# A graph network kernel: sums by source begun in the scatter stage, in chunks of 384 rows, and a first stage with less in it

## The chip, the cores and the metric

One core of one Trainium2 chip runs the whole program in one launch. The metric is the device time of that launch in microseconds (us). Times in the trace count from the start of the profiled span. PE is the engine for matrix products (PEld its weight loads), DVE the vector engine, ACT the activation engine, POOL the GpSimd engine, SP the engine that only issues DMAs here.

## The reference, cut to what matters

The graph has N = 3125 nodes and E = 53125 directed edges with 128 features each; `dst` is sorted, `src` is not. Four graph layers run one after the other. The change touches the preparation of the first two, which need for each node the sum of the edge rows that start in it and the sum of those that end in it:

```
edge_aggr = jnp.zeros((x.shape[0], edge_attr.shape[1]), dtype=x.dtype)
edge_aggr = edge_aggr.at[row].add(edge_attr).at[col].add(edge_attr)     # row = src, col = dst
node_features = jnp.concatenate([x, edge_aggr], axis=1)
h = jax.nn.relu(node_features @ W1 + b1)
```

Before each layer the node rows are normalised (mean and variance over the 128 features), which is why statistics of x are made in the same preparation.

## The kernel before, in words

The edges are 415.04 tiles of 128, handled as 416 tiles: 208 pairs of tiles, or 104 groups of four tiles (`PAIRS`, `GROUPS`). The nodes are 25 blocks of 128. There are four stretches of interest, each closed by a barrier of all engines.

**First stage** (lines 410 to 520). Constants, index tables, clearing of the big tables, the first loads of edge rows. ACT and POOL clear `between`, a table of 20000 words per partition: POOL in two memsets of 2800 and 9400 words (L456, L458), ACT the other 7800 (L440). DVE makes the tables from the indices; PE turns them and then runs 16 products of ones (`stream_ones`, L380), which serve no result. SP loads edge rows into a ring of eight groups and issues the large DMA that zeroes the end of each block's place in DRAM (L426, L429), then the last four of the ring's loads.

**Scatter stage** (`place_and_count`). For each group, PE works out the place of each edge row in a table in DRAM that is kept by the block of its source node (`rank`, L897 to L901). DVE reads the ranks (`own_rank`, L830), ACT turns the base of the next group out of PSUM (`base_of_next`, L789), DVE turns ranks into places (`place`, `place_whole`, L839), and POOL writes the rows to those places, four indirect DMAs to a group (L765). For each pair, DVE makes wide one-hots (`hots`, L817), ACT narrow ones (`lows`, L782 and L785), PE multiplies them (L917 to L926), and DVE adds the product to `between` and `by_dst` two pairs later (`collect`, L849 and L851). ACT writes the key of a row beside it (`key_in_row`, L775). Each engine runs a list in program order. `which_block` of DVE (L824) waits for the newest rank, and `rank` waits for the base that ACT makes. Every pair begins on PE with products of ones: 3 of them, in every 32nd pair 16.

**Stage of the sums by source** (`sum_blocks`). The rows of each block are read back from DRAM, 18 tiles of 128 rows for each of 24 blocks and 9 for the last: 441 tiles in 74 reads of up to six, in a ring of four buffers. SP issues a read when PE has finished with the buffer (L1101), DVE makes a one-hot of the keys (`where`, L1120), PE adds up (L1170), DVE adds the sum by destination (`add_dst`, L1112). Beside it DVE makes the statistics of x (L1063, L1136), and ACT checks the 25 blocks of `between` (L1153).

**The rest** (from L1187 on): the four layers. The change leaves it as it is, except that some of its semaphores are shared with a branch that isn't taken.

Of the kernel before, what the change touches and what calls it, by code (L numbers as in the profile page):

```python
# [12 lines left out]
F32 = mybir.dt.float32  # L13
# [66 lines left out]
WARM_SHORT = 12  # L80
LAST_BANK = 7
WARM_EVERY = 32


class Signal:
# [6 lines left out]
    def __init__(self, make):  # L92
        self.make, self.on_path, self.base = make, {}, {}

    @property
    def h(self):
        branch = Signal.path is not None
        if branch not in self.on_path:
            self.on_path[branch] = self.make()
        return self.on_path[branch]  # L100
# [44 lines left out]
def build(nc, x, src, dst, ea, l0, l1, l2, l3, out):  # L145
    ctx = ExitStack()
    with ctx:
# [7 lines left out]
        def signal(name):  # L155
# [3 lines left out]
            return Signal(make)  # L159
# [95 lines left out]
        bounds = sb("bounds", [1, 2, NB])  # L255
        over = sb("over", [1, 2, NB])
# [22 lines left out]
        tab_row = sb("tab_row", [1, 2, 2, ST * P], I32)  # L279
        tab_bc = sb("tab_bc", [P, 2, 2, ST * P])  # L280

        shifts = [sb(f"shift{k}", [P, SLOTS_OF[k], GS[k]]) for k in range(2)]
# [15 lines left out]
        junk = grid_space.take([P, NP], U8)  # L298
        excess = grid_space.take([P, NB])
# [91 lines left out]
        POOL_FIRST, POOL_SECOND = 2800, 9400  # L391
# [18 lines left out]
        with nc.Block() as block:  # L410
            @on(block.sync)
            def _(sp):
# [18 lines left out]
                for g in range(EARLY, ROWG):  # L431
                    load_group(sp, g)

            @on(block.scalar)
            def _(act):
# [77 lines left out]
            def _(pe):  # L513
# [8 lines left out]
                stream_ones(pe, LAST_BANK, WARM_UP)  # L522
# [126 lines left out]
        pair_done = signal("pair_done")  # L649
        taken = signal("taken")  # L650
# [68 lines left out]
        def place_and_count():  # L719
# [15 lines left out]
            with nc.Block(no_gpsimd_drain=True) as block:  # L735
                @on(block.sync)
                def _(sp):
                    for g in range(ROWG, GROUPS):
# [6 lines left out]
                        if g == 6 * ROWG:  # L745
                            sp.wait_ge(vec.h, vec.at(1))
                            sp.dma_start(x_nm[:, 0:NB - 1, :], x[0:(NB - 1) * P, :].rearrange("(b p) f -> p b f", p=P)).then_inc(loaded.h, 16)
                            sp.dma_start(x_nm[0:NLAST, NB - 1, :], x[(NB - 1) * P:N, :]).then_inc(loaded.h, 16)
                    sp.wait_ge(loaded.h, loaded.at(16 * 23))
# [19 lines left out]
                def _(act):  # L769
# [16 lines left out]

                    def base_of_next(g):
                        act.wait_ge(ranks_read.h, ranks_read.at(g + 1))
                        act.activation(bases[:, (g + 1) % 2, :], acc[0:1, R_AT + RANKS:R_AT + RANKS + NK], ACT.Copy).then_inc(based.h, 1)  # L789
# [4 lines left out]
                    for i in range(PAIRS):  # L794
# [4 lines left out]
                        if i % PG == 1 and g + 1 < GROUPS:  # L799
                            base_of_next(g + 1)  # L800

                @on(block.vector)
                def _(dve):
# [54 lines left out]
                    for i in range(PAIRS + 2):  # L858
                        g = i // PG
                        if i % PG == 0 and g < GROUPS:  # L860
                            place(g)
                        if i < PAIRS:
                            hots(i)
                        if i % PG == 0 and g < GROUPS:
# [7 lines left out]
                        if i == 4 * ROWG * PG:  # L872
                            dve.wait_ge(tail_zero.h, tail_zero.at(32))
                            dve.memset(x_nm[:, NB - 1, :], 0.0).then_inc(vec.h, 1)
                    dve.memset(odd[:, 3:4], 0.0)
                    dve.tensor_scalar(bounds[:, 0, 0:NB - 1], iota[0:1, 0:NB - 1], float(CAP), float(FILLED), ALU.mult, ALU.add)
# [1717 lines left out]
```

## Time and profile before

| | |
|---|---|
| median of 3 runs | 1464.97 us (1463.71 to 1466.68) |
| the profiled execution's own time | 1461.87 us |
| its span | 1460.0 us |
| first stage | 0 to 22.6 us |
| scatter stage | 22.6 to 558.7 us |
| stage of the sums by source | 558.7 to 685.4 us |
| the rest | 685.4 to 1460.0 us |

The stages follow each other with barriers, so what one stage is shortened or lengthened by moves everything behind it. Within a stage the engines run side by side, and the stage is as long as the one that ends last.

### The profile page before, as it was taken

Reading aid. Unit: us, or ns where it says so; the run is one execution under the profiler, and the core shown is the slowest. Engines: PE = TensorE matmul, PEld = TensorE weight load, DVE = VectorE, ACT = ScalarE, POOL = GpSimd, SP = SyncE. Lnnn points to the kernel's source line nnn. Section 1 sums busy time; section 2 is a strip of 40 time slices with the busy share of each in tenths; the row PEclk is TensorE's granted clock in tenths of the full one; section 3 lists DMA queues with packets and bytes.
Section 4 is the critical chain, followed back from the end, with each engine's and each line's share of the span. In section 5 each row is a group of like instructions: output and inputs, shape, how many; then the busy total and the mean of one; then the engine's idle time right before and its main releaser. Section 6 shows DMA issues by size and latency. Waiting matters only on the chain. (4 is left out here: it accounts for less than half of the span.)

```text
span 1460.0 us, 32667 instructions
## 1 busy us (share of the span) xinstructions
PE 1248.2 (85%) x9632; PEld 906.7 (62%) x9633; DVE 880.1 (60%) x2762; ACT 554.3 (38%) x1458; POOL 808.4 (55%) x844
## 2 busy tenths in 40 slices
PE   5888888888888887887789998999988898988986
PEld 3555555555555556886469996477766666666664
DVE  6777777787877876665785448244444433443434
ACT  5444544444445447940241104233322222222221
POOL 5777777777777771000000001777777777777770
PEclk9999999999999999999799998899999999999996
DMA  7533335333333325875500003655555555455422
GB/s 230 135 104 106 104 108 148 101 104 104 103 108 108 102 67 177 240 240 162 48 1 2 1 2 105 166 153 154 158 155 154 154 151 142 136 149 142 134 75 56
DMA packets 198505, 174.71 MB, mean 120 GB/s; under 512 B 48724, under 2 KB 171078, under 8 KB 198246
## 3 DMA queue, kind: packets, MB, share of 16 engines
q1 hardware_dynamic: 171752, 118.36, 30.1%
q0 software_dynamic: 26624, 54.79, 13.0%
q8 instruction: 61, 1.00, 0.3%
q14 instruction: 68, 0.56, 0.2%
HBM read 134.89 MB, written 38.16 MB: 119 GB/s over the span
## 5 line engine op out<-in xcount | busy, mean ns | idle before, releaser
L2132 POOL DMA_INDIRECT between<-p_table,src_g x416 | 397.2, 955 | 474.1 <-DMA p_table<-n_nm 347.6
L380 PE MATMUL acc<-ones_b 128*128 128x512 bf16 x1606 | 426.3, 386 | 31.4 <-PEq L1396 12.4
L765 POOL DMA_INDIRECT rows_by_block<-h_t,mean_bc x312 | 299.8, 961 | 109.7 <-issue 77.4
L380 PEld LDWEIGHTS acc<-ones_b 128*128 128x128 bf16 x1606 | 142.5, 99 | 132.6 <-issue 39.0
L917 PE MATMUL acc<-n_nm 128*128 128x384 bf16 (+1 forms) x832 | 140.8, 291 | 86.6 <-DVE n_nm L817 85.8
L2204 ACT ACTIVATE between<-acc 128x256 f32<-128x256 f32 x208 | 79.8, 383 | 355.3 <-PE acc L2252 348.2
L849 DVE TENSOR_TENSOR between<-between,acc 128x600 f32 x208 | 161.3, 775 | 61.5 <-issue 49.8
L2163 DVE TENSOR_TENSOR between<-acc,between 128x256 f32<-128x256 f32 x208 | 87.8, 422 | 169.2 <-DMA between<-p_table,src_g 108.6
L2277 PE MATMUL acc<-w_msg,between 128*128 128x128 f32 x832 | 185.5, 305 | 0.0
L2263 PEld LDWEIGHTS acc<-between 128*128 128x128 f32 x832 | 129.6, 198 | 82.6 <-issue 58.9
L2263 PE MATMUL acc<-between 128*128 128x24 f32 x832 | 134.6, 243 | 49.5 <-DVE agg_sum L2172 49.0
L917 PEld LDWEIGHTS acc<-n_nm 128*128 128x128 bf16 x832 | 66.3, 97 | 163.5 <-DVE n_nm L817 134.3
L817 DVE TENSOR_SCALAR n_nm<-iota_w,agg_sum 128x600 bf16<-128x600 f16 x416 | 153.5, 409 | 0.0
L782 ACT ACTIVATE away<-iota_b,agg_sum 128x128 bf16<-128x128 bf16 x416 | 140.8, 385 | 0.0
L2277 PEld LDWEIGHTS acc<-w_msg,between 128*128 128x128 f32 x832 | 127.0, 193 | 0.1
L789 ACT ACTIVATE bases<-acc 1x26 f32<-1x26 f32 x104 | 18.9, 182 | 265.1 <-DVE agg_sum L830 262.8
L1170 PE MATMUL acc<-n_nm,h_t 128*128 128x128 f32 x882 | 108.2, 280 | 12.7 <-DVE n_nm L1120 12.2
L765 POOL DMA_INDIRECT rows_by_block<-agg_sum,mean_bc x104 | 99.7, 959 | 32.5 <-issue 25.5
L2252 PE MATMUL acc<-ident,between 128*128 128x128 f32 x416 | 114.3, 276 | 0.0
L1170 PEld LDWEIGHTS acc<-n_nm,h_t 128*128 128x128 f32 x882 | 101.7, 192 | 19.4 <-DVE n_nm L1120 18.9
L2172 DVE TENSOR_TENSOR agg_sum<-agg_sum,acc 128x24 f32 x208 | 37.4, 180 | 117.8 <-issue 60.1
L785 ACT ACTIVATE n_nm<-away,ones 128x256 bf16<-128x256 bf16 x208 | 105.6, 508 | 6.8
(194 smaller groups left out, 1942.7 us busy)
## 6 DMA issues: line engine op xcount, KB each, us to landing
h_t<-rows_by_block SPq DMA_DIRECT2D x73, 387.0 KB, 3.7
between<-in_edge_attr SPq DMA_DIRECT2D x207, 128.0 KB
h_t<-in_edge_attr SPq DMA_DIRECT2D x78, 256.0 KB
between<-in_dst SPq DMA_DIRECT2D x51, 288.0 KB
between<-p_table,src_g POOLq DMA_INDIRECT x416
agg_sum<-in_edge_attr SPq DMA_DIRECT2D x25, 256.0 KB
rows_by_block<-h_t,mean_bc POOLq DMA_INDIRECT x312
rows_by_block<-x_nm SPq DMA_DIRECT2D x1, 4644.0 KB, 18.6
```

Source lines behind the costliest of these rows:

```text
L380: pe.matmul(acc[:, bank * BANK:(bank + 1) * BANK].rearrange("p (a n) -> p a n", n=P), ones_b[:, :], ones_b[:, :].rearrange("p (a n) -> p a ...
L765: pool.indirect_dma_start(rows_by_block, bass.IndirectOffsetOnAxis(ap=place_in_table[:, t:t + 1], axis=0), row_group(g)[:, j, :], None).th ...
L782: act.activation(away[:, h + j, :], iota_b[:, :], ACT.Abs, scale=-1.0, bias=lo_s[:, 2 * i + j:2 * i + j + 1])\
L785: act.activation(low_hot[:, h:h + 2, :], away[:, h:h + 2, :], ACT.Relu, scale=-1.0, bias=ones[:, 0:1]).then_inc(lows_made.h, 1)
L817: ins = dve.tensor_scalar(wide_hot[:, i % HOTB * 2 + j, :], iota_w[:, :], key_w[:, t:t + 1], None, ALU.is_equal)
L849: dve.tensor_tensor(between[:, :, bass.ds(first, W)], between[:, :, bass.ds(first, W)], acc[:, o:o + NB * WS].rearrange("p (b w) -> p b w" ...
L917: pe.matmul(acc[:, to:to + (b1 - b0) * WS].rearrange("p (b w) -> p b w", w=WS)[:, :, 0:W], low_hot[:, h + j, :], wide_hot[:, h + j, b0 * W ...
L1170: last = pe.matmul(acc[:, o:o + P], rows_in_block[:, q, j, 0:D], hot_in_block[:, q, j, :], start=is_first and j == 0, stop=is_last and j = ...
L2132: pool.indirect_dma_start(got[:, q, j * D:(j + 1) * D], None, p_table, bass.IndirectOffsetOnAxis(ap=src_g[:, n * G + j:n * G + j + 1], axi ...
L2252: last = pe.transpose(acc[:, o:o + P], rows[:, i, j, :], ident[:, :])
L2263: last = pe.matmul(acc[:, o:o + W], relued[:, i % MR, j, :], onehot[:, i * G + j, :], start=j == 0, stop=j == G - 1)
L2277: last = pe.matmul(acc[:, o:o + P], turned[:, i % MR, j * P:(j + 1) * P], w_msg[:, 2, :], start=False, stop=True)
```

## The change: what it does

1. In the scatter stage, from group 29 on, the first 9 of the 18 tiles of each of 24 blocks are read back and summed while later rows are still being scattered. A chunk is 3 tiles (384 rows) of one block, 72 chunks in all, one to a group. SP loads it (`load_chunk`), ACT makes its one-hot (`hots_of_chunk`: three Abs and one Relu), PE sums it (`sum_chunk`) and ACT copies the result out of PSUM to `home` (`take_chunk`). In the second and third round over the blocks PE first adds what `home` already holds, by a product with the identity.
2. PE's list there: `rank` comes ahead of the products of ones; they go to the bank of the pair, behind the wait for it (`taken`); a pair with a chunk has 1 of them, not 3.
3. The stage of the sums reads 225 tiles in 50 reads, not 441 in 74. The load of x moves into it from the scatter stage. DVE adds `by_dst` to `home` there once (3072 words) and joins the last 11 blocks of `between` by ten bitwise ors of 800 words, so that ACT checks 15 blocks, not 25. PE starts it with 6 products of ones, not 16.
4. First stage: POOL clears in 26 pieces of 400 words without waiting for anyone, ACT 9600 words, not 7800; 12 products of ones, not 16; the last four ring loads go to the next stage.
5. The first group's `place_whole` comes ahead of its one-hots on DVE.

```diff
+CT = 3
+CROWS = CT * P
+CRING, CHOTS = 3, 2
+CHUNK_LOAD, CHUNK_HOT, CHUNK_SUM, CHUNK_TAKE = 32, 29, 30, 31
+CHUNKS = EC // KC - CHUNK_LOAD
+BY_CHUNK = [min(NB - 1, CHUNKS - c * (NB - 1)) for c in range(-(-CHUNKS // (NB - 1)))]
...
-        POOL_FIRST, POOL_SECOND = 2800, 9400
+        POOL_PIECE, POOL_PIECES = 400, 26
...
-                clear(between_words[:, POOL_FIRST + POOL_SECOND:])
+                clear(between_words[:, POOL_PIECE * POOL_PIECES:])
...
-                pool.wait_ge(vec.h, vec.at(6))
-                pool.memset(between_words[:, 0:POOL_FIRST], 0.0)
-                pool.wait_ge(idx_read.h, idx_read.at(1))
-                pool.memset(between_words[:, POOL_FIRST:POOL_FIRST + POOL_SECOND], 0.0)
+                for k in range(POOL_PIECES):
+                    pool.memset(between_words[:, k * POOL_PIECE:(k + 1) * POOL_PIECE], 0.0)
...
-                stream_ones(pe, LAST_BANK, WARM_UP)
+                stream_ones(pe, LAST_BANK, WARM_SHORT)
...
+                    def load_chunk(m):
+                        if m >= CRING:
+                            sp.wait_ge(chunk_summed.h, chunk_summed.at(m + 1 - CRING))
+                        row = m % (NB - 1) * CAP + m // (NB - 1) * CROWS
+                        sp.dma_start(chunk_rows[:, m % CRING, :, :], rows_by_block[row:row + CROWS, :].rearrange("(p j) w -> p j w", j=CT))\
+                          .then_inc(chunk_in[m % CRING].h, 16)
...
+                    def hots_of_chunk(m):
+                        act.wait_ge(chunk_in[m % CRING].h, chunk_in[m % CRING].at(16 * (m // CRING + 1)))
+                        if m >= CHOTS:
+                            act.wait_ge(chunk_summed.h, chunk_summed.at(m + 1 - CHOTS))
+                        h = chunk_hot[:, m % CHOTS, :, :]
+                        for j in range(CT):
+                            act.activation(h[:, j, :], iota[:, :], ACT.Abs, scale=-1.0, bias=chunk_rows[:, m % CRING, j, D:KW]).then_inc(chunk_away.h, 1)
+                        act.wait_ge(chunk_away.h, chunk_away.at(CT * (m + 1)))
+                        act.activation(h, h, ACT.Relu, scale=-1.0, bias=ones[:, 0:1]).then_inc(chunk_hots.h, 1)
+
+                    def take_chunk(m):
+                        act.wait_ge(chunk_summed.h, chunk_summed.at(m + 1))
+                        o, b = IDLE_BANK * BANK, m % (NB - 1)
+                        act.activation(home[:, b * P:b * P + P], acc[:, o:o + P], ACT.Copy).then_inc(chunk_taken.h, 1)
...
                             base_of_next(g + 1)
+                        if i % PG == 1 and 0 <= g - CHUNK_HOT < CHUNKS:
+                            hots_of_chunk(g - CHUNK_HOT)
+                        if i % PG == 0 and 0 <= g - CHUNK_TAKE < CHUNKS:
+                            take_chunk(g - CHUNK_TAKE)
...
+                    def sum_chunk(m):
+                        pe.wait_ge(chunk_hots.h, chunk_hots.at(m + 1))
+                        if m >= 1:
+                            pe.wait_ge(chunk_taken.h, chunk_taken.at(m))
+                        o = IDLE_BANK * BANK
+                        again = m >= NB - 1
+                        if again:
+                            b = m % (NB - 1)
+                            pe.matmul(acc[:, o:o + P], ident[:, :], home[:, b * P:b * P + P], start=True, stop=False)
+                        for j in range(CT):
+                            last = pe.matmul(acc[:, o:o + P], chunk_rows[:, m % CRING, j, 0:D], chunk_hot[:, m % CHOTS, j, :],
+                                             start=j == 0 and not again, stop=j == CT - 1)
+                        last.then_inc(chunk_summed.h, 1)
...
-                        stream_ones(pe, IDLE_BANK, WARM_UP if i % WARM_EVERY == WARM_EVERY - 1 else WARM_PAIR)
                         if c == 0 and g + 1 < GROUPS:
                             rank(g + 1)
+                        with_chunk = c == 0 and 0 <= g - CHUNK_SUM < CHUNKS
+                        if with_chunk:
+                            sum_chunk(g - CHUNK_SUM)
+                        if i >= PRING:
+                            pe.wait_ge(taken.h, taken.at(i + 1 - PRING))
+                        stream_ones(pe, at_bank(i) // BANK, WARM_UP if i % WARM_EVERY == WARM_EVERY - 1 else WARM_CHUNK if with_chunk else WARM_PAIR)
...
+                done = CT * sum(b < k for k in BY_CHUNK)
+                for j in range(done, n, LR):
...
+                        if r == 2:
+                            dve.tensor_tensor(home[:, 0:(NB - 1) * P], home[:, 0:(NB - 1) * P], agg_dst[:, 0:(NB - 1) * P], ALU.add)
```

**PE, one group of the scatter stage.** Before the change PE's list for a group reads as follows (L380 are the products of ones, L897 to L901 the rank, L917 to L926 the products of a pair).

```order
L380 MATMUL acc<-ones_b 128x512 x3
L897 MATMUL acc<-bases,ones 128x130
L888 MATMUL acc<-agg_sum,ones_b 128x104
L888 MATMUL acc<-agg_sum,ones_b 128x78
L888 MATMUL acc<-agg_sum,ones_b 128x52
L888 MATMUL acc<-agg_sum,ones_b 128x26
L901 MATMUL acc<-agg_sum,lower_b 128x104
L917 MATMUL acc<-n_nm 128x16x24 x2
L917 MATMUL acc<-n_nm 128x9x24 x2
L923 MATMUL acc<-agg_sum 128x24 x2
L926 MATMUL acc<-agg_sum,ones_b 128x24 x2
```

With the change, in a group of the second and third round over the blocks (L952 to L956 are the rank, L966 the identity product, L968 the chunk, L395 the ones, L989 on the pair):

```order
L952 MATMUL acc<-bases,ones 128x130
L943 MATMUL acc<-agg_sum,ones_b 128x104
L943 MATMUL acc<-agg_sum,ones_b 128x78
L943 MATMUL acc<-agg_sum,ones_b 128x52
L943 MATMUL acc<-agg_sum,ones_b 128x26
L956 MATMUL acc<-agg_sum,lower_b 128x104
L966 MATMUL acc<-home,ident 128x128
L968 MATMUL acc<-x_nm 128x128 x3
L395 MATMUL acc<-ones_b 128x512
L989 MATMUL acc<-n_nm 128x16x24 x2
L989 MATMUL acc<-n_nm 128x9x24 x2
```

The rank has moved to the front, and the chunk stands between it and the pair's own products, in place of two of three products of ones.

**ACT, one group of the scatter stage.** Before (L789 is the base, L782 and L785 the one-hots of a pair, L775 the key):

```order
L789 ACTIVATE bases<-acc 1x26
L782 ACTIVATE away<-iota_b,agg_sum 128x128 x2
L785 ACTIVATE n_nm<-away,ones 128x256
L775 ACTIVATE h_t<-agg_sum 128x4
L782 ACTIVATE away<-iota_b,agg_sum 128x128 x2
L785 ACTIVATE n_nm<-away,ones 128x256
```

With the change (L833 is the base, L819 and L821 the chunk's one-hot, L808 and L811 the pair's, L801 the key, L826 the copy of the chunk of the group before):

```order
L833 ACTIVATE bases<-acc 1x26
L819 ACTIVATE x_nm<-iota,x_nm 128x128 x3
L821 ACTIVATE x_nm<-x_nm,ones 128x384
L808 ACTIVATE away<-iota_b,agg_sum 128x128 x2
L811 ACTIVATE n_nm<-away,ones 128x256
L801 ACTIVATE h_t<-agg_sum 128x4
L826 ACTIVATE home<-acc 128x128
L808 ACTIVATE away<-iota_b,agg_sum 128x128 x2
L811 ACTIVATE n_nm<-away,ones 128x256
```

The one-hot of the chunk that PE sums next stands ahead of the pair's one-hots, and the copy of the chunk before it stands behind them.

**DVE, the stage of the sums, its sixth to eighth read.** With the change (L1208 makes the one-hot of a read, L1228 is a bitwise or, L1200 adds the sum by destination):

```order
L1208 TENSOR_TENSOR n_nm<-iota,h_t 128x384
L1228 TENSOR_TENSOR mean_bc<-between 128x800
L1208 TENSOR_TENSOR n_nm<-iota,h_t 128x768
L1228 TENSOR_TENSOR mean_bc<-mean_bc,between 128x800
L1200 TENSOR_TENSOR agg_sum<-acc,home 128x128
L1208 TENSOR_TENSOR n_nm<-iota,h_t 128x384
L1228 TENSOR_TENSOR mean_bc<-mean_bc,between 128x800
```

Reads of six and of three tiles alternate, and each of ten reads is followed by an or, where before each read had six tiles and a short statistics instruction behind it in the middle part.

## Rows read from the trace of the kernel before

**Rows 1.** Busy us (x instructions) per engine, granted clock, DMA share, GB/s; three stages.

```profile
0.00:22.64 22.64, 8.33 (x26) 3.74 (x27) 14.85 (x30) 13.42 (x4) 11.70 (x12) 1.00 0.90 282
22.64:558.75 536.11, 442.40 (x3510) 274.96 (x3511) 417.48 (x1308) 255.88 (x832) 399.53 (x416) 1.00 0.37 107
558.75:685.37 126.62, 113.17 (x898) 103.52 (x898) 84.06 (x162) 78.00 (x53) 0.00 (x0) 0.99 0.77 231
```

**Rows 2.** Timeline, first stage: start, us, engine, line, what, idle before.

```profile
7.00 7.93 POOL L458 MEMSET between<- 128x9400 f32 x1 [0.60 <-DVE n_nm L489]
7.46 6.69 ACT L440 ACTIVATE between<-ones 128x7800 f32<-128x7800 f32 x1
8.80 6.24 DVE L492 TENSOR_SCALAR win_f<-mean_bc 1x208 f32<-1x208 f32 x1
...
16.09 5.12 PE L380 MATMUL acc<-ones_b 128*128 128x512 bf16 x16
...
17.99 4.23 SPq L405 DMA_DIRECT2D agg_sum<-in_edge_attr  x2
...
22.66 0.44 DVE L824 TENSOR_TENSOR agg_sum<-iota,agg_sum 128x104 bf16<-128x104 f32 x2 [3.14 <-PEq L410]
```

**Rows 3.** Timeline of POOL: its first and its last (416th) scatter.

```profile
26.22 1.15 POOL L765 DMA_INDIRECT rows_by_block<-h_t,mean_bc  x1 [11.29 <-ACT h_t L775]
...
555.71 0.96 POOL L765 DMA_INDIRECT rows_by_block<-agg_sum,mean_bc  x1 [0.31 <-issue]
```

**Rows 4.** Timeline, one group of the scatter stage with PE, DVE and ACT.

```profile
520.13 0.29 PEld L897 LDWEIGHTS acc<-bases,ones 1*128 1x128 f32 x2 [0.42 <-issue]
520.70 0.21 PE L901 MATMUL acc<-agg_sum,lower_b 128*128 128x104 bf16 x1
520.80 0.67 PE L917 MATMUL acc<-n_nm 128*128 128x384 bf16 x4
520.95 0.27 DVE L824 TENSOR_TENSOR agg_sum<-iota,agg_sum 128x104 bf16<-128x104 f32 x1 [0.59 <-PE acc L901]
...
521.74 0.81 PE L380 MATMUL acc<-ones_b 128*128 128x512 bf16 x3
...
523.95 0.26 DVE L830 TENSOR_TENSOR agg_sum<-acc,agg_sum 128x104 f32<-128x104 f32 x1
524.24 0.18 ACT L789 ACTIVATE bases<-acc 1x26 f32<-1x26 f32 x1 [2.31 <-DVE agg_sum L830]
...
524.32 0.68 ACT L782 ACTIVATE away<-iota_b,agg_sum 128x128 bf16<-128x128 bf16 x2
...
525.03 0.51 ACT L785 ACTIVATE n_nm<-away,ones 128x256 bf16<-128x256 bf16 x1
...
525.45 0.19 ACT L775 ACTIVATE h_t<-agg_sum 128x4 f32<-128x4 f32 x1
```

**Rows 5.** Timeline, a late POOL start, and a pair with 16 products of ones.

```profile
506.74 0.76 DVE L849 TENSOR_TENSOR between<-between,acc 128x600 f32 x1
...
507.53 0.95 POOL L765 DMA_INDIRECT rows_by_block<-agg_sum,mean_bc  x1 [1.10 <-issue]
...
510.18 3.61 PE L380 MATMUL acc<-ones_b 128*128 128x512 bf16 x16
```

**Rows 6.** Lines in the stage of the sums: count, busy us, mean ns, idle before.

```profile
L1120 DVE TENSOR_TENSOR n_nm<-iota,h_t 128x768 f32<-128x768 f32 x74 | 70.4, 951 | 42.1 <-DMA h_t<-rows_by_block 41.8
...
L1214 ACT ACTIVATE w_msg<-acc 128x128 f32<-128x128 f32 x1 | 0.3, 277 | 2.8 <-PE acc L1206 2.8
```

**Rows 7.** Timeline, stage of the sums: first read, PE on a read, last read.

```profile
561.85 0.96 DVE L1120 TENSOR_TENSOR n_nm<-iota,h_t 128x768 f32<-128x768 f32 x1 [1.45 <-DMA h_t<-rows_by_block]
...
569.32 1.41 PEld L1170 LDWEIGHTS acc<-n_nm,h_t 128*128 128x128 f32 x12 [0.25 <-DVE n_nm L1120]
...
683.09 0.56 DVE L1120 TENSOR_TENSOR n_nm<-iota,h_t 128x384 f32<-128x384 f32 x1 [1.26 <-DMA h_t<-rows_by_block]
```

**Rows 8.** Windows: the thinnest five us of PE in the sums.

```profile
645.00:650.00 5.00, 3.38 (x28) 3.00 (x26) 2.29 (x6) 0.00 (x0) 0.00 (x0) 1.00 0.83 242
```

More of the change, by code:

```diff
@@ L254, in build @@
         bases = sb("bases", [1, 2, NK])
-        bounds = sb("bounds", [1, 2, NB])
-        over = sb("over", [1, 2, NB])
+        chunk_space = Space(x_nm[:, :, :].rearrange("p b f -> p (b f)")[:, (CAP - FILLED) // P * KW if FILLED else 6 * KW:], F32)
+        chunk_rows = chunk_space.take([P, CRING, CT, KW])
+        chunk_hot = chunk_space.take([P, CHOTS, CT, P])
+        bounds = chunk_space.take([1, 2 + len(BY_CHUNK), NB])
+        over = chunk_space.take([1, 2 + len(BY_CHUNK), NB])
+        counts_at = chunk_space.take([1, len(BY_CHUNK), NB])
         low_bound = sb("low_bound", [P, 1])
@@ L276, in build @@
         b1_row = sb("b1_row", [P, H2])
-        tab_row = sb("tab_row", [1, 2, 2, ST * P], I32)
-        tab_bc = sb("tab_bc", [P, 2, 2, ST * P])
-        shifts = [sb(f"shift{k}", [P, SLOTS_OF[k], GS[k]]) for k in range(2)]
+        home = sb("home", [P, NP])
+        general_space = Space(home[:, :], F32)
+        tab_row = general_space.take([1, 2, 2, ST * P], I32)
+        tab_bc = general_space.take([P, 2, 2, ST * P])
+        shifts = [general_space.take([P, SLOTS_OF[k], GS[k]]) for k in range(2)]
         win_f = sb("win_f", [1, PAIRS])
@@ L649, in build @@
         pair_done = signal("pair_done")
+        chunk_in = [signal(f"chunk_in{q}") for q in range(CRING)]
+        chunk_away = signal("chunk_away")
+        chunk_hots = signal("chunk_hots")
+        chunk_summed = signal("chunk_summed")
+        chunk_taken = signal("chunk_taken")
         taken = signal("taken")
@@ L861, in _ @@
                             place(g)
+                        if i == 0:
+                            place_whole(g)
                         if i < PAIRS:
                             hots(i)
-                        if i % PG == 0 and g < GROUPS:
+                        if i % PG == 0 and 0 < g < GROUPS:
                             place_whole(g)
@@ L873, in _ @@
                             dve.wait_ge(tail_zero.h, tail_zero.at(32))
+                            dve.memset(over[:, :, :], 0.0)
                             dve.memset(x_nm[:, NB - 1, :], 0.0).then_inc(vec.h, 1)
                     dve.memset(odd[:, 3:4], 0.0)
+                    for c, n in enumerate(BY_CHUNK):
+                        dve.tensor_scalar(bounds[:, 2 + c, 0:n], iota[0:1, 0:n], float(CAP), float((c + 1) * CROWS), ALU.mult, ALU.add)
                     dve.tensor_scalar(bounds[:, 0, 0:NB - 1], iota[0:1, 0:NB - 1], float(CAP), float(FILLED), ALU.mult, ALU.add)
@@ L883, in _ @@
                     dve.tensor_tensor(over[:, 1, :], bases[:, GROUPS % 2, 0:NB], bounds[:, 1, :], ALU.is_gt)
+                    for c, n in enumerate(BY_CHUNK):
+                        dve.tensor_tensor(over[:, 2 + c, 0:n], counts_at[:, c, 0:n], bounds[:, 2 + c, 0:n], ALU.is_lt)
                 @on(block.tensor)
@@ L937, in place_and_count @@
             away_made.passed(EC)
-            loaded.passed(16 * 23)
+            for s in (chunk_hots, chunk_summed, chunk_taken):
+                s.passed(CHUNKS)
+            chunk_away.passed(CT * CHUNKS)
+            for q in range(CRING):
+                chunk_in[q].passed(16 * len(range(q, CHUNKS, CRING)))
+            loaded.passed(16 * 21)
             vec.passed(2)
@@ L1151, in _ @@
                 def _(act):
-                    for b in range(NB):
-                        act.activation(junk[:, :], between[:, b, :], ACT.Relu, bias=low_bound[:, :], accum_out=excess[:, b:b + 1]).then_inc(checked.h, 1)
-                        if b < NB - 1:
+                    for b in range(ALONE + 1):
+                        if b == ALONE:
+                            act.wait_ge(united.h, united.at(NB - ALONE - 1))
+                        of = between[:, b, :] if b < ALONE else mean_bc[:, 2 * EC:2 * EC + NP // 4].bitcast(U8)
+                        act.activation(junk[:, :], of, ACT.Relu, bias=low_bound[:, :], accum_out=excess[:, b:b + 1]).then_inc(checked.h, 1)
+                        if b < ALONE:
                             act.wait_ge(checked.h, checked.at(b + 1))
```

109 lines of the change are left out of this document (70 added, 39 removed).

## The prediction

> **What bounds the kernel now.** I read the table by stage first, then the timeline inside each stage that the change touches. The table [rows 1] gives 22.64 us to the first stage, 536.1 to the scatter stage, 126.6 to the sums by source; the rest is left alone. The first stage ends with SP: its last two loads run from 17.99 for 4.23 us, to 22.22, and DVE begins the next stage at 22.66 [rows 2]. Before that DVE lost time: an instruction on 208 elements took 6.24 us and ended at 15.04, just behind POOL's 9400-word memset, which ended at 14.93 [rows 2].
>
> In the scatter stage POOL is busy 399.5 us and runs from 26.22 to 555.71 + 0.96 = 556.67 [rows 1, 3]. That is 530.45 us for 416 scatters, 1.275 each with the 0.30 us that stands before one, so 5.10 us to a group. POOL never rests, and bounds the stage. But PE, DVE and ACT are close behind. The group shown [rows 4] is one link of a loop: PE's rank (from 520.13 to 520.91) lets DVE go on, DVE's chain ends with L830 at 524.21, ACT's base follows at 524.24. A change that puts work into this loop must be judged by the loop and not by ACT's 255.9 us of 536 [rows 1].
>
> In the stage of the sums DVE waits 41.8 us for rows [rows 6], DMA moves 231 GB/s [rows 1], and reads follow each other every (683.09 - 561.85)/73 = 1.66 us [rows 7]. The reads bound it.
>
> **First stage.** SP's last loads leave it. What is left: ACT's clearing, 6.69 us for 7800 words from 7.46 [rows 2], becomes 6.69 x 9600/7800 = 8.23 and ends at 15.7. PE's last burst of ones has 12 and not 16, and begins some 6 us earlier. DVE no longer sits behind one memset, but each of its instructions may meet a piece: 7.93 x 400/9400 = 0.34 us. From 15.04 (end of the stalled one) DVE has work until 19.5 (estimate: 22.66 less its idle 3.14 [rows 2]), 4.5 us, and without the stall it would begin this near 9.3; with ten meetings at half to a whole piece it ends at 15.5 to 17. I take 16.6 for the last engine and 17.0 for the next stage's start: 5.6 us earlier. Bounds: 16.1 (ACT alone) and 22.6 (nothing gained). The moved loads are wanted only from group 4 on, some 20 us into the stage; they are issued at its start and cost nothing. The Trainium skill, SBUF — State Buffer, section "SBUF: two separate sides", says that DVE in a two-port mode and POOL take a shared port pair for a whole instruction; the trace agrees in the 6.24 us above, and by that rule a piece of 0.34 us is the most that one meeting costs.
>
> POOL began 3.56 us after the stage did (26.22 against 22.66); `place_whole` ahead of the first one-hots takes about the 0.67 us of two of them off. POOL begins at 19.9.
>
> **Scatter stage.** Per chunk ACT gains three Abs, a Relu on 384, and a copy; PE gains three tiles and from the 25th chunk on an identity product, and loses two products of ones. Counted as work ACT would hold: it waits 2.31 us before each base [rows 4]. But the order makes a longer loop. `sum_chunk(m)` on PE waits for `take_chunk(m-1)`. That copy stands on ACT behind the base, the chunk's one-hot, one pair's one-hots and the key. On PE the chunk stands ahead of both pairs of the group, and the next rank stands behind them. From a rank to the rank two groups on, this must be walked through:
> - DVE from rank to L830: 524.21 - 520.91 = 3.30 [rows 4].
> - ACT from L830 to the end of the copy: 0.03 to the base and 0.08 to the next start; three Abs 1.01 (0.71 from the first of two to the Relu [rows 4], one more 0.30); Relu on 384: 0.42 for 256 (525.03 to 525.45 [rows 4]) and 0.12 for 128 more, 0.54; the pair's one-hots 0.71 + 0.42; key 0.10; copy 0.28 as L1214 [rows 6]; 0.05 to PE. Together 3.22.
> - PE from there to the rank after next: three tiles 0.70 (12 loads for six tiles in 1.41 us [rows 7]), one product of ones 0.22 (3.61/16 [rows 5]), a pair 0.94 (520.80 to 521.74 [rows 4]), three ones 0.68, a pair 0.94, 0.05, the rank 0.78. Together 4.31, with the identity product 0.235 more, 4.55.
>
> The sum is 10.83 us for two groups, 5.42 a group, and 5.53 with the identity. POOL needs 5.10. So over 72 groups not POOL but this loop sets the pace: 24 x 5.42 + 48 x 5.53 = 395.5 us. In five of these groups (every 16th) stands the pair with 16 ones; 13 x 0.225 = 2.9 us each, now on the path, 14.6 together. PE waits in each such group, about 1.1 us before the chunk.
>
> The groups without a chunk get quicker, since the ones stand behind the rank now. Their shortest loop is 3.30 + 0.03 + 0.18 + 0.05 + 0.78 = 4.34 us; POOL's pace, at which they go now, is 5.10. I take 4.7. In 30 such groups the three engines run ahead of POOL, which later eats up this lead. The last group's places are ready at 19.9 + 30 x 4.7 + 2 (one burst) + 395.5 + 14.6 + 4.7 = 577.7, and with its four scatters (5.04) POOL ends at 582.7: 26.0 us later than the 556.67 of before. Left out as hidden: SP's chunk loads (half a read of six tiles to a group, issued two groups ahead; DMA share is 0.37 [rows 1] and would be near 0.5), and the small bounds and counts of DVE and ACT.
>
> Bounds: the free pace 4.34 to 5.10 (-10.8, +12); ACT's part 0.3 either way (0.15 x 72 = 10.8 either way), since no row has an Abs or a Relu of these shapes.
>
> **Stage of the sums.** 225 of 441 tiles, 50 reads not 74, and x (3125 rows of 512 bytes, 1.6 MB) more. From below: the stage moved 231 GB/s x 126.6 = 29.2 MB; 225/441 of it is 14.9, with x 16.5, at 240 GB/s (231 to 242 [rows 1, 8]) 69 us, with 3.1 before the first read (561.85 - 558.75) and 2 behind the last, 74. From above: 50 reads at the 1.66 us of the larger ones, 83, and 5, 88. DVE: 84.1 us [rows 1] less 24 reads of 0.951 and 25 that shrink from 0.951 to 0.56, less 32.6, plus ten ors of 800 at about 0.99 ((0.951 - 0.56)/384 us an element) and one sum of 3072 at 3.3, gives 65; it comes close to the reads in the part with the ors. I take 80, nearer the middle: 46.6 less than 126.6.
>
> **Sum.** 1461.87 + 26.0 - 46.6 = 1441.3 (the 5.6 of the first stage is inside the 26.0). The median of before lies 3.1 over the profiled execution; so 1444.
>
> **The rivals.**
> *POOL still bounds the scatter stage.* If the copy and one-hots of a chunk cost less than half of what I put, or the lead is enough, POOL runs 530.45 us from 19.9 on to 550.4, 6.3 earlier than before. 1461.87 - 6.3 - 46.6 + 3.1 = 1412. For it: ACT's 2.31 us of waiting [rows 4]. Against: the wait for the copy is in the code, and 5.42 stands against 5.10.
>
> *POOL's pieces starve DVE in the first stage.* 26 x 0.34 is 8.8 us back to back; if DVE gets no gap, the stage is as long as before: 5.6 more, 1450.
>
> *ACT's part is longer.* Each 0.1 us on it adds 0.05 x 72 = 3.6. With 0.6 more: 1444 + 21.6 = 1466, and nothing is gained.
>
> *DVE blocks POOL, slower.* A scatter began 0.80 us late (1.10 of idle for 0.30) and began when DVE's L849 (506.74 + 0.76 = 507.50) was over, at 507.53 [rows 5]. Now the two keep step, and this is rare. If DVE out of step blocks one scatter in each group, POOL needs 5.10 + 0.80 = 5.90, in 104 groups 613.6, to 633.5: 1461.87 + 76.8 - 46.6 + 3.1 = 1495. It decides from 0.51 us a group on (583.4/104 = 5.61). Against it: of the 530.45 us all but some 6 are 416 x (0.96 + 0.30). The Trainium skill tells of this in SBUF — State Buffer, "SBUF: two separate sides": a DVE instruction in a two-port mode keeps the cores of GpSimd from writing DMA descriptors. [...]
>
> *PE's clock falls in the thinner sums.* PE would be busy near two thirds of the time. The thinnest five us of before had 3.38 busy at clock 1.00 [rows 8], which speaks against it. At half speed 225 tiles of 2 x 0.235 are 106 us, with 5 more 111: 1444 + 31 = 1475.
>
> **How the numbers follow.** The forecast as summed 0.74; POOL bound 0.08; starved DVE 0.08; longer ACT part 0.05; blocked POOL 0.03; clock 0.02. The forecast's own range, from its bounds taken together (11, 11, 7 and 2 us, root of squares 17 to 19), is 1426 to 1462. Leaving out half of the extremes on both sides the range is 1417 to 1463; POOL-bound and blocked POOL lie outside. A measurement tells 0.2%, 2.9 us, from no change: faster (below 1462.0) 0.86, within 0.07, slower 0.07.
>
> **What would show it.** Right: in groups 30 to 101 POOL idles 0.3 to 0.5 us more per group, and the rank follows the rank by 5.4 to 5.5 us; PE waits for ACT before the chunk; ACT hardly waits for L830; before group 30 scatters lag behind their places. The next stage begins near 17, the sums near 585, and last 80. Wrong: scatters every 1.26 us to the end; PE's wait before the chunk absent; a stage of the sums over 90 or under 72 us.

## The result, and the profile after

The changed kernel takes 1486.36 us (median of 4 runs, 1484.47 to 1488.85), the kernel before beside it 1465.83 (1463.71 to 1469.23): ratio 1.0139, 95% interval 1.0112 to 1.0166. It is slower by 20.5 us where 1444 was forecast, and it lies outside the range. The profiled execution's own time is 1488.85, its span 1487.0.

The windows of the changed kernel, by its three stages (columns as in [rows 1]):

```profile
0.00:22.14 22.14, 8.41 (x22) 3.52 (x23) 17.58 (x30) 14.92 (x4) 11.04 (x36) 1.00 0.88 289
22.14:629.80 607.66, 511.66 (x3894) 369.97 (x3895) 401.75 (x1315) 375.03 (x1195) 400.98 (x416) 0.92 0.41 115
629.80:714.46 84.66, 64.44 (x456) 57.31 (x456) 61.90 (x150) 47.44 (x33) 0.00 (x0) 0.92 0.65 196
```

The first stage gives 0.5 us (22.64 - 22.14), the scatter stage costs 71.5 (607.66 - 536.11), the sums give 42.0 (126.62 - 84.66), the rest, 772.5 us, gives 2.1: together the span is 27.0 us longer (1487.0 against 1460.0). The granted clock of the scatter stage is 0.92, where it was 1.00, and POOL is as busy as before.

The first stage, from the timeline of the changed kernel:

```profile
1.91 9.75 POOL L469 MEMSET between<- 128x400 f32 x26
2.60 9.15 DVE L492 CAST iota<-iota_i 128x128 f32<-128x128 int32 x1
2.73 9.01 DVE L493 CAST part<-part_i 128x1 f32<-128x1 int32 x1
...
7.47 8.19 ACT L453 ACTIVATE between<-ones 128x9600 f32<-128x9600 f32 x1
...
16.56 5.30 PE L395 MATMUL acc<-ones_b 128*128 128x512 bf16 x12
```

Both casts end by 11.75, just behind the last of 26 pieces (1.91 + 9.75 = 11.66). DVE's whole chain begins only then. The twelve ones wait for it, begin at 16.56 (16.09 before) and end at 21.86, and with them the stage. They take 0.44 us each, twice the 0.22 of [rows 5], and so 5.30 together, more than the 5.12 of the sixteen before.

Timeline of POOL in the changed kernel, its first and last scatter:

```profile
25.00 1.15 POOL L791 DMA_INDIRECT rows_by_block<-h_t,mean_bc  x1 [13.34 <-ACT h_t L801]
...
626.79 0.95 POOL L791 DMA_INDIRECT rows_by_block<-agg_sum,mean_bc  x1 [0.30 <-issue]
```

The run of the scatters is 627.74 - 25.00 = 602.7 us; 562.8 were forecast (582.7 - 19.9), and 530.45 it was [rows 3].

Waits of the changed kernel: who waited for what, us in total, times, longest:

```profile
POOL rows_by_block L791 <- DVE mean_bc L887: 83.7, 41, 6.7
...
PE acc L966 <- ACT home L826: 51.5, 24, 2.2
...
PE acc L968 <- ACT home L826: 25.3, 12, 2.4
```

PE waits for the copy `home` 36 times in 72 chunks, 76.8 us in all, 2.13 each: in every second group. POOL in turn waits 83.7 us for its places, which in the kernel before were 5.8 us between 24 and 550. Two groups in the timeline of the changed kernel (L956 ends a rank, L826 is the copy, L966 and L968 the chunk, L989 and L995 a pair, L395 the ones):

```profile
395.85 0.48 PE L952 MATMUL acc<-bases,ones 1*128 1x130 f32 x2
...
396.42 0.21 PE L956 MATMUL acc<-agg_sum,lower_b 128*128 128x104 bf16 x1
...
397.64 0.67 PE L989 MATMUL acc<-n_nm 128*128 128x384 bf16 x4
...
400.81 0.21 PE L956 MATMUL acc<-agg_sum,lower_b 128*128 128x104 bf16 x1
...
402.78 0.26 ACT L826 ACTIVATE home<-acc 128x128 f32<-128x128 f32 x1
...
403.18 0.46 PE L966 MATMUL acc<-home,ident 128*128 128x128 f32 x2 [2.16 <-ACT home L826]
...
404.64 1.21 PE L989 MATMUL acc<-n_nm 128*128 128x384 bf16 x4
...
405.64 0.92 PE L995 MATMUL acc<-agg_sum,h_t 128*128 128x24 f32 x4
...
406.46 1.29 PE L395 MATMUL acc<-ones_b 128*128 128x512 bf16 x3
...
408.60 0.48 PE L952 MATMUL acc<-bases,ones 1*128 1x130 f32 x2
```

The short group takes 4.39 us (396.42 to 400.81). In the long one PE stands idle for 2.16 us (a stand, below) and then makes the pair's products in 1.21 us, not 0.67. A rank's first product is 396.42 - 395.85 = 0.57 ahead of its L956, so the one begun at 408.60 has it at 409.17: 8.36 us, and 12.75 for both, where 11.07 were forecast. The windows of the same stretch show the clock:

```profile
402.00:404.00 2.00, 0.82 (x7) 0.85 (x8) 2.00 (x6) 1.94 (x7) 1.60 (x2) 1.00 0.11 35
404.00:406.00 2.00, 2.00 (x11) 1.30 (x10) 1.64 (x8) 1.78 (x7) 1.49 (x2) 0.51 0.35 60
406.00:408.00 2.00, 2.00 (x11) 1.15 (x12) 0.00 (x0) 1.97 (x8) 1.39 (x3) 0.63 0.83 272
408.00:410.00 2.00, 2.00 (x23) 1.85 (x22) 0.27 (x1) 0.52 (x2) 1.70 (x2) 1.00 0.21 66
```

PE is on its lower level, 1.2 GHz, in nearly all of the window behind the stand and most of the next, and back at 2.4 GHz in the last.

Not every stand is followed by this. The long group just before, and the windows there:

```profile
389.70 0.21 PE L956 MATMUL acc<-agg_sum,lower_b 128*128 128x104 bf16 x1
...
392.06 0.46 PE L966 MATMUL acc<-home,ident 128*128 128x128 f32 x2 [2.16 <-ACT home L826]
...
393.25 0.67 PE L989 MATMUL acc<-n_nm 128*128 128x384 bf16 x4
```

```profile
392.00:394.00 2.00, 1.94 (x16) 1.71 (x17) 1.97 (x7) 1.78 (x7) 1.70 (x2) 1.00 0.20 66
394.00:396.00 2.00, 2.00 (x19) 1.48 (x19) 0.56 (x3) 1.94 (x6) 1.39 (x3) 1.00 0.84 231
```

The stand is the same 2.16 us, but the pair's products take 0.67, and the group is over in 6.72 us (389.70 to 396.42): 11.11 for it and the short one behind it, which is the 11.07 of the forecast. Over the stage, the first pair behind a stand took 0.67 us in 14 of the 36 cases, 1.20 or 1.21 in 18, and something between in four. From one L956 to the next, 22 long groups take 1.4 to 2.95 us more than those at full clock do (6.50 early in the stage, 6.72 later; 9.3 and 9.52 where the sixteen ones stand), 42.95 us together. Without these the run of the scatters would be 602.74 - 42.95 = 559.8 us.

### The profile page after: what moved, and what is told of

It is laid out like the page before. It is cut to its first block and busy times, and to the rows that moved or that the text cites. A ratio compares the mean times of both kernels' runs of the same rounds, so it can differ in the third digit from the quotient of the medians.

```text
span 1487.0 us, 33072 instructions
## 1 busy us (share of the span) xinstructions
PE 1271.7 (86%) x9570; PEld 958.7 (64%) x9571; DVE 843.9 (57%) x2757; ACT 644.2 (43%) x1801; POOL 810.2 (54%) x868
## 5 line engine op out<-in xcount | busy, mean ns | idle before, releaser
L395 PE MATMUL acc<-ones_b 128*128 128x512 bf16 x1448 | 412.3, 403 | 32.3 <-PEq L1507 11.7
L395 PEld LDWEIGHTS acc<-ones_b 128*128 128x128 bf16 x1448 | 136.5, 102 | 130.9 <-issue 43.7
L897 DVE TENSOR_TENSOR between<-between,acc 128x600 f32 x208 | 161.5, 776 | 60.1 <-issue 56.8
L989 PE MATMUL acc<-n_nm 128*128 128x384 bf16 (+1 forms) x832 | 155.6, 314 | 0.1
L865 DVE TENSOR_SCALAR n_nm<-iota_w,agg_sum 128x600 bf16<-128x600 f16 x416 | 144.3, 388 | 0.0
L989 PEld LDWEIGHTS acc<-n_nm 128*128 128x128 bf16 x832 | 85.8, 105 | 86.2 <-issue 28.8
L808 ACT ACTIVATE away<-iota_b,agg_sum 128x128 bf16<-128x128 bf16 x416 | 141.1, 387 | 0.0
L833 ACT ACTIVATE bases<-acc 1x26 f32<-1x26 f32 x104 | 18.9, 182 | 214.7 <-DVE agg_sum L878 214.7
L872 DVE TENSOR_TENSOR agg_sum<-iota,agg_sum 128x104 bf16<-128x104 f32 x104 | 27.8, 268 | 142.4 <-PE acc L956 139.5
L811 ACT ACTIVATE n_nm<-away,ones 128x256 bf16<-128x256 bf16 x208 | 105.6, 508 | 6.8
L2387 PE MATMUL acc<-between 72*128 72x128 bf16 x416 | 91.4, 220 | 0.0
```

What stands on the lines that cost most here:

```text
L395: pe.matmul(acc[:, bank * BANK:(bank + 1) * BANK].rearrange("p (a n) -> p a n", n=P), ones_b[:, :], ones_b[:, :].rearrange("p (a n) -> p a ...
L808: act.activation(away[:, h + j, :], iota_b[:, :], ACT.Abs, scale=-1.0, bias=lo_s[:, 2 * i + j:2 * i + j + 1])\
L811: act.activation(low_hot[:, h:h + 2, :], away[:, h:h + 2, :], ACT.Relu, scale=-1.0, bias=ones[:, 0:1]).then_inc(lows_made.h, 1)
L865: ins = dve.tensor_scalar(wide_hot[:, i % HOTB * 2 + j, :], iota_w[:, :], key_w[:, t:t + 1], None, ALU.is_equal)
L897: dve.tensor_tensor(between[:, :, bass.ds(first, W)], between[:, :, bass.ds(first, W)], acc[:, o:o + NB * WS].rearrange("p (b w) -> p b w" ...
L989: pe.matmul(acc[:, to:to + (b1 - b0) * WS].rearrange("p (b w) -> p b w", w=WS)[:, :, 0:W], low_hot[:, h + j, :], wide_hot[:, h + j, b0 * W ...
```

## The experiments

**Theory.** Two things were paid: the loop through the copy of the chunk before, as forecast; and the lower clock behind many of the stands of 2.2 us, which wasn't. **Rival:** the loop alone, or the clock for want of work in all.

**The copy first.** ACT takes the chunk before at the head of a group, ahead of the base, and not behind the one-hots.

```diff
+                        if i % PG == 1 and 0 <= g - CHUNK_SUM < CHUNKS:
+                            take_chunk(g - CHUNK_SUM)
                         if i % PG == 1 and g + 1 < GROUPS:
                             base_of_next(g + 1)
...
-                        if i % PG == 0 and 0 <= g - CHUNK_TAKE < CHUNKS:
-                            take_chunk(g - CHUNK_TAKE)
```

> One move in ACT's list of the changed kernel: the copy of a chunk (take_chunk) stands ahead of the base of the same group's second pair, where ACT waits anyway, and no longer behind the next chunk's one-hot and a pair's one-hots. Theory of the loop (PE waits for the copy, then loses clock): the walk from a rank to the rank two groups on falls to 3.30 + 2.94 + 3.39 = 9.6 us, 4.8 a group, below POOL's 5.10; POOL runs 530 us from 25.0 on, PE no longer stands still before a chunk, its clock stays at 1.00 in the scatter stage, and the time is near 1414. Rival, DVE or the chunk loads hold POOL back: scatters go on having gaps, the scatter stage stays over 570 us and the time over 1450.

Measured: 1419.37 us (1416.94 to 1421.29), ratio to before 0.9672 (0.9635 to 0.9709). The waits of PE for `home` are gone (what is left is 39 waits for the chunk's one-hot, 24.4 us, the longest 1.1), and so is POOL's for its places (4.6 us in all). The windows of its stage show the clock at 0.98; it is 1.00 from 100 to 500 and 0.88 from 500 to 550, where PE runs out of work:

```profile
180.00:555.50 375.50, 328.38 (x2745) 243.77 (x2742) 278.11 (x892) 286.46 (x903) 283.84 (x294) 0.98 0.46 135
```

Its last scatter, in the timeline:

```profile
552.43 0.96 POOL L791 DMA_INDIRECT rows_by_block<-agg_sum,mean_bc  x1 [0.30 <-issue]
```

The scatters run 553.39 - 25.00 = 528.4 us: POOL bounds again. One place on ACT's list was worth 67 us (1486.36 - 1419.37); 1414 was expected.

**Ones in the wait.** ACT's list stays as in the changed kernel; PE gets five products of ones where it stood, and none behind. The wait for the pair's bank moves ahead of the chunk with them.

```diff
-                        if with_chunk:
-                            sum_chunk(g - CHUNK_SUM)
...
-                        stream_ones(pe, ..., WARM_CHUNK if with_chunk else WARM_PAIR)
+                        stream_ones(pe, ..., 5 if with_chunk else WARM_PAIR)
+                        if with_chunk:
+                            sum_chunk(g - CHUNK_SUM)
```

> The changed kernel, but a pair with a chunk has its products of ones (5, not 1) between the rank and the wait for the chunk, and none behind it: PE still waits for the copy, but is busy for 1.1 us of the wait. Theory that the clock makes the part of the loss that the sum of durations lacks: the clock stays near 1.00 in groups 30 to 101, groups follow each other every 5.3 to 5.5 us without a long one in two, the scatter stage takes some 555 to 565 us, the time is near 1440. Rival, the loop is longer for another reason than the clock: the stage stays near 600 us and the time near 1480.

Measured: 1446.63 us (1443.55 to 1451.25), ratio 0.9864 (0.9824 to 0.9904). The windows of the scatter stage:

```profile
180.00:576.00 396.00, 381.26 (x3024) 269.05 (x3024) 279.41 (x894) 285.57 (x904) 282.33 (x294) 1.00 0.46 128
```

PE in the timeline, three ranks that follow each other:

```profile
395.80 0.21 PE L956 MATMUL acc<-agg_sum,lower_b 128*128 128x104 bf16 x1
395.84 1.24 PE L395 MATMUL acc<-ones_b 128*128 128x512 bf16 x5
...
401.33 0.21 PE L956 MATMUL acc<-agg_sum,lower_b 128*128 128x104 bf16 x1
...
406.69 0.21 PE L956 MATMUL acc<-agg_sum,lower_b 128*128 128x104 bf16 x1
```

More products of no use, and 40 us less. The clock is 1.00, and two groups take 10.89 us (395.80 to 406.69). The forecast's 11.07 has a product of ones of 0.22 behind the chunk, which this kernel doesn't have on the path; without it 10.85 were forecast. The scatters run from 23.77 to 576.30, 552.5 us, 24 over the copy-first kernel. Of the 50.2 us to the changed kernel's 602.7, some 8 (an estimate: 36 x 0.22) are that product, and some 42 the clock, which agrees with the 42.95 counted above.

**Three ones behind the chunk** (`WARM_CHUNK = 3`). It tells the stand from want of work in all. It ran first on a chip on which the kernel before takes 1868.8 us (more on this below), and again on another beside the changed kernel.

> The changed kernel, with 3 products of ones in a pair with a chunk in place of 1, in their place behind the chunk. Theory A: PE's clock falls because of the stand of 2.2 us ahead of the chunk in every second group, which these ones don't shorten. Then the clock stays at 0.92 to 0.93, the loop has up to 0.45 us more for two groups, 72/2 x 0.45 = 16 us, and the time is 1490 to 1502. Rival: the clock falls because PE does too little in all in these groups; two more products a pair bring it back to 0.96, and with some 40 us less from the clock and 16 more of products the time is 1455 to 1470.

> The changed kernel with 3 products of ones behind the chunk, beside the changed kernel on one chip. As before: where the stand ahead of the chunk is what lowers the clock, the time is 0 to 16 us over the changed kernel's and the clock no higher; where PE's whole work in these groups is what counts, it is 15 to 30 us under it and the clock 0.95 or more.

> The changed kernel once more, so that the next run has it on its own chip. 1.014 of the kernel before on either chip.

Measured, all on one chip, with before at 1463.78: three ones 1505.06 (1502.6 to 1507.92), changed kernel again 1484.92 (1480.37 to 1488.4, ratio 1.0147, 1.0115 to 1.0178). PE was busy for 33.8 us more between 180 and the last scatter (391.47 against 357.70), and the clock there was 0.91 against 0.92. Timeline with three ones:

```profile
400.43 0.46 PE L966 MATMUL acc<-home,ident 128*128 128x128 f32 x2 [1.72 <-ACT home L826]
...
401.54 1.49 PE L395 MATMUL acc<-ones_b 128*128 128x512 bf16 x3
402.82 1.21 PE L989 MATMUL acc<-n_nm 128*128 128x384 bf16 x4
...
405.28 0.67 PE L989 MATMUL acc<-n_nm 128*128 128x384 bf16 x4
```

Ones behind the chunk don't help: the stand stays (35 of them, most of 1.7 to 2.1 us), the pair's products behind it came slow in 23 cases, and there the ones run at half speed themselves. In the changed kernel one such product took 0.63 us behind the stand, here three take 1.49: 0.86 more in 36 long groups bounds it at 31 us from above, and 20 were lost (1505.06 - 1484.92), 4 more than the 16 that were put as the most. The rival, which had 15 to 30 us less, falls. On the other chip the ratio was 1.0136 (1.0078 to 1.0194), with no changed kernel beside it.

**The order of PE alone.** The kernel before, with the rank ahead of the ones, and the ones in the pair's bank behind `taken`.

> The kernel before with PE's list changed alone: the rank ahead of the products of ones, these in the pair's own bank behind the wait for it. No chunks, first stage and sums as before. POOL bounds the stage, so the time stays within 0.2% of before (1463 to 1468); places should run ahead of their scatters by several groups at the end if the quicker loop (4.3 to 4.7 us a group) is real, and by 3 us as before if POOL's pace binds DVE through another way.

Measured: 1462.95 us, ratio 0.9970 (0.9947 to 0.9994). Part 2 of the change costs nothing and brings next to nothing; the cost is in the chunks. The quicker loop is real: in this trace the last L901 stands at 523.05, 33 us ahead of the end of the last scatter, where it was 11 before (545.48 and 556.67). In the changed kernel the groups ahead of the chunks go at 4.50 us (29 from 23.05 to 153.51), where 4.7 were taken.

**POOL's clearing as before, with the copy first.**

```diff
+                pool.wait_ge(vec.h, vec.at(6))
+                pool.memset(between_words[:, 0:2800], 0.0)
+                pool.wait_ge(idx_read.h, idx_read.at(1))
+                pool.memset(between_words[:, 2800:POOL_PIECE * POOL_PIECES], 0.0)
```

> As the kernel with the copy moved forward, and POOL clears its 10400 words in two memsets with the waits of the kernel before, 2800 and 7600, not in 26 pieces from the start. Theory that the pieces hold DVE off for all of their 9.75 us: DVE makes its first tables at once again, is held by the second memset alone, to about 14, and the next stage begins near 20 and not at 22.1: 2 us less than with the pieces. Rival, the pieces cost nothing: the same time.

Measured: 1418.9 us (1417.28 to 1421.58), ratio 0.9666 (0.9627 to 0.9704). The first scatter comes at 23.65, not 25.00: the twelve ones, 5.30 us in both, begin at 15.21 and not at 16.56. The 1.35 us can't be told in the median, and the ones alone vary by as much: in the kernel with ones in the wait, whose first stage is that of the changed kernel, the same twelve took 4.07 us and the first scatter came at 23.77. DVE is still held once: its L505 on 208 elements took 4.75 us beside the memset of 7600 words.

**Pieces behind the casts, and pieces alone.** First the copy-first kernel in which POOL waits for the table casts ahead of its 26 pieces; then the kernel before with nothing but the 26 pieces and ACT's 9600 words.

> The order of the take-first kernel, and POOL begins its 26 pieces of 400 words only when DVE's three table casts are done (near 3.9 us). Theory A: pieces that stand back to back hold DVE off as one memset does, because no gap between them is long enough for a DVE instruction to begin. Then the casts take their short times, but the next DVE instruction of the kind that stalls (the one on 208 elements behind PE's first transposes, or the cast of 1024 before it) takes up to the end of the 26 pieces at 3.9 + 26 x 0.375 = 13.7 us. Rival: the pieces let DVE in between, and only the bunch of the first casts was unlucky: then each DVE instruction takes at most 0.4 us more and the chain ends near 14. The first scatter comes at 23 to 24 us by A, near 20 by the rival; the time is 1419 by A, 1414 by the rival.

> The kernel before with one edit: POOL clears in 26 pieces of 400 words from the start without waiting, and ACT 9600 words instead of 7800. Theory A: the pieces starve DVE by themselves: the first cast behind them takes some 9 us and ends with the last piece at 11.7, DVE's chain ends about where it did, and the scatter stage starts within 1 us of 22.7; the time is that of the kernel before within 0.2%. Rival: it was the rest of the change (the casts' order, the moved loads) that held DVE; then the chain runs free and the stage starts when the last ring load lands, near 22, with DVE done by 17.

Timeline of the first, first stage:

```profile
3.44 0.47 DVE L498 CAST iota_w<-n_nm 128x600 f16<-128x600 int32 x1
3.96 9.78 POOL L470 MEMSET between<- 128x400 f32 x26 [2.00 <-DVE iota_w L498]
5.88 8.40 DVE L501 CAST n_nm<-n_nm 128x1024 f32<-128x1024 int32 x1 [1.98 <-DMA n_nm<-in_dst]
```

The casts are short now, and the next one pays: 8.40 us for what took 0.68 in the changed kernel. It ends at 14.28, 0.54 behind the last piece, and the first scatter comes at 25.88, later than the 23 to 24 expected. So the pieces gave DVE no turn. Pieces alone: both casts took 9.14 and 9.01 us there too, ratio 1.0022 (0.9991 to 1.0053), no change, as the theory had it.

These runs fell on another chip, on which the kernel before takes 1868.8 us, and the copy-first kernel with this edit has a ratio of only 0.996 (0.9928 to 0.9992). In the scatter stage (24 to 754) the clock was 0.79 with pieces alone. Its timeline:

```profile
289.93 0.27 DVE L822 TENSOR_TENSOR agg_sum<-iota,agg_sum 128x104 bf16<-128x104 f32 x1 [5.10 <-remote]
...
292.26 1.18 PE L915 MATMUL acc<-n_nm 128*128 128x384 bf16 x4 [5.19 <-DVE n_nm L815]
```

DVE stood 5.10 us with no releaser inside the kernel, PE with it, and PE's products took 1.18 us, not 0.67. What makes these stands isn't known here, there is no trace of the kernel before from that chip, and medians from it decide nothing about a few us.

**x in pieces.** The copy-first kernel again; in the stage of the sums x comes in six pieces of four blocks, one behind every second read.

```diff
-                        if r == LB_IN:
+                        if LB_IN <= r < LB_IN + 12 and (r - LB_IN) % 2 == 0:
...
-                            sp.dma_start(x_nm[:, 0:NB - 1, :], x[0:(NB - 1) * P, :]...)
+                            sp.dma_start(x_nm[:, k6:k6 + 4, :], x[k6 * P:(k6 + 4) * P, :]...)
```

> The order of the take-first kernel, and in the stage of the sums the load of x cut into six pieces of four blocks and the last block's rows, one piece behind every second read from the fifth on. Theory A: the stage takes 86.5 us where 80 were forecast, because DVE waits 5.4 us for the first read that is queued behind the whole load of x, and that wait isn't made up. Then the stage gets 3 to 5 us shorter: some 82 us, and the time falls to 1415. Rival: the stage is bound by its total of bytes and by DVE's list behind it; then the long wait goes, short ones come, the stage stays at 86 us and the time at 1419.

On the slower chip the reads of this stage were issued from 792.7 to 867.6, 74.9 us, those of the kernel with the casts first, with the whole load, from 786.1 to 867.4, 81.3; the time was 1864.68, ratio 0.9969 (0.9938 to 0.9999). Last, all three edits together (copy first, POOL's clearing as before, x in pieces), beside the copy-first kernel:

> The take-first order, POOL's two memsets behind their waits, and x in pieces. By the trace of the pieces on the slower chip the stage of the sums is 4 to 7 us shorter than with the whole load; the scatter stage is POOL's. On a chip that runs the kernel before at 1466 us: 1419 - 5 = 1414. Rival: the shorter stage is taken back by the stage behind it, whose first work waits for something else; then 1419. On a chip with the lower clock (the kernel before at 1868 us) the ratio is 0.99 to 1.00.

> The take-first kernel once more, beside the changed kernel on one chip. On a chip that runs the kernel before at 1466 us: 1419 again, 67 us under the changed kernel. On a chip with the lower clock PE is slower in both, and POOL waits for the loop of rank, DVE, ACT and rank in both; the copy taken early still spares the loop what PE waits: 10 to 25 us under the changed kernel, ratio to the kernel before near 1.00.

Measured: all three 1413.82 us (1413.27 to 1416.11), ratio 0.9661 (0.9645 to 0.9678); copy first 1420.69 (1417.24 to 1422.71), ratio 0.9702 (0.9679 to 0.9724). The difference of 6.9 us holds both other edits: 1.6 is the earlier first scatter (22.50 against 24.07). What the load of x does in the changed kernel, first in the timeline of SP:

```profile
636.96 3.29 SPq L1189 DMA_DIRECT2D x_nm<-in_x  x1
```

Then in that of DVE:

```profile
646.19 0.56 DVE L1208 TENSOR_TENSOR n_nm<-iota,h_t 128x384 f32<-128x384 f32 x1 [5.37 <-DMA h_t<-rows_by_block]
```

A read queued behind it keeps DVE waiting for 5.37 us. In pieces, the stage lasts from 554.0 to 636.3, 82.3 us; with the whole load from 555.4 to 643.0, 87.6. The seven traces with the whole load on the faster chips lie between 84.7 and 87.9. This is the best version measured, 50.0 us under the kernel before on its chip.

## Why the prediction was wrong

*What bounds the kernel* was read rightly. The loop had been seen, with the rule that it must be judged by the loop and not by ACT's busy time, and where the clock stood at 1.00 it held: 11.11 us for two groups of the changed kernel against 11.07, 10.89 against 10.85 with the ones in the wait. Less the time lost behind stands, the run of scatters is 559.8 us in both profiles of the changed kernel (602.74 - 42.95, and 592.39 - 32.61), 562.8 in the forecast. The identity product, the Abs and the Relu were priced well: three Abs take 0.97 to 1.01, the Relu 0.52 to the next start, for 1.01 and 0.54.

**The step that failed** is in the scatter stage: the walk through the loop priced every product at full clock, and said that "PE waits in each such group, about 1.1 us before the chunk". The waits bunch instead: none in one group, 2.13 us in the next. Behind 22 of the 36 such stands PE works at half clock for a while, the rank is late, and two groups take 12.75 us and more, not 11.11. This is 42.95 us in the first profile and 32.6 in the second (20 stands). It is nearly the whole miss of 42, and the sign. It was shown from both sides: filled stand, full clock, 40 us less in the median (1486.36 - 1446.63), of which some 8 are the product of ones that left the path; filled elsewhere, no gain. Why the clock fell behind one stand and not behind the next of the same 2.16 us stays open.

**The rival on the clock** was set up in the wrong stage. It looked at the sums, where PE is thin, and put 31 us and 2% on it. The row of before against it [rows 8] had PE busy 3.38 of 5 us in many short gaps; it says nothing on one long stand. In the sums the clock fell too, from 0.99 to 0.92; what that cost there no run isolates.

**The first stage** gave 0.5 us, not 5.6. The rival of the starved DVE, at 8%, is what came: "each of its instructions may meet a piece", at 0.34 us a meeting, was the wrong step. Behind it the ones were priced too low: twelve took as long as sixteen. The next stage began at 22.14 instead of 17.0, a miss of 5.1. The Trainium skill's SBUF — State Buffer, "SBUF: two separate sides", was read as freeing the shared port behind each piece; a row of 9.15 us beside pieces of 9.75/26 = 0.375 us shows that this cast got no turn between pieces that follow back to back.

**The stage of the sums** took 84.7 us, not 80: mis-sized by 4.7. The 5.37 us of DVE behind the load of x are of that size, and in pieces 5.3 us came back.

*POOL still bounds*, 1412, is what the copy placed first makes of it: 1419. *Longer ACT part* didn't come. *DVE blocks POOL* rests on a row that doesn't show it. The scatter at 507.53 is the 378th, and in the trace of before the 114th, 202nd, 290th and 378th begin 0.8 to 1.4 us late, always 88 apart. In the changed kernel the 202nd, 290th and 378th are late too, by 1.1 us, and DVE has been idle for more than 2 us when they are due (its L872 at 433.47 comes after 3.75 us of waiting):

```profile
433.15 0.96 POOL L791 DMA_INDIRECT rows_by_block<-h_t,mean_bc  x1 [1.41 <-issue]
```

So it goes by the number of the scatter and not by DVE. With the copy first all of them are on time; what makes the delay stays open. The rest of POOL's waiting is for places.

Added up from the 1441.3 forecast for the profiled execution: clock +42.95, loop -3.0 (559.8 for 562.8), first scatter +5.1 (25.00 for 19.9), sums +4.7, the rest -2.1 give 1488.9; its time was 1488.85.

## What to carry to other kernels

When a loop between engines is priced, price TensorE at both clock levels, and look for the longest single stand, not the mean gap: a stand of 2.2 us cost up to 2.9 us more behind it. A result that the next turn needs is copied out at the head of the list of its engine, not behind the work of this turn. Work of no use belongs into the stand and not behind it; and a long load is cut up where short ones queue behind it.

## What the runs showed of the hardware that wasn't expected

- Cutting a POOL memset into pieces of 0.375 us doesn't let DVE in: casts took 9.15 and 8.40 us, each ending within 0.6 us of the end of the 26th piece. In the kernel before, a copy out of PSUM (128x416, 0.59 us at 8.18) passed beside the 9400-word memset unhindered.
- Stands of 1.26 to 2.45 us, most of 2.16, with PE at work on both sides, were followed by half clock in 22 of 36 cases, in whole or in part (0.51 granted in the two us behind the one at 403.18), and by full clock in the rest. The kernels whose longest waits of PE there were 0.8 and 1.1 us kept a clock of 1.00 from 180 to 500; the changed kernel had 0.88 and 0.92 there in its two profiles.
- Of the chips used one ran the same kernel 27% slower (1868.8 against 1465.8 us), with stands of some 5 us in its traces that nothing in the kernel released; the copy first was worth 3.3% on the one, and with POOL's wait 0.4% on the other.
